# Memory attention: where a pair's second batch is weighted, and what turns the first pair's values and probabilities

## What is computed

```python
xn  = layernorm(x) * ln_g + ln_b              # (32, 512)
q   = split_heads(xn @ Wq)                    # 16 heads of 64
kv  = xn @ Wkv
mem = split_heads(memories @ Wm)              # memories = context, 257 rows
k   = concat([kv[:, :1024] heads, mem])       # 32 + 257 = 289 keys
v   = concat([kv[:, 1024:] heads, mem])       # the same mem is keys and values
attn = softmax(q @ k.T / 8)
out = (attn @ v) @ Wo + bo                    # added to x
```

## Time and profile before

| | us |
|---|---|
| runs of the kernel (3) | 2068.11, 2071.55, 2072.27; median 2071.55 |
| profiled execution, its time | 2070.35 |
| its span, first to last instruction | 2068.6 |
| mean granted TensorE clock | 0.984 |
| PE / DVE / ACT busy | 1985.6 / 1229.0 / 882.2 |
| the loop over pairs | about 1314.8 to 1860 |

### The profile page before, as it was taken

The page is one execution under the profiler, slowest core; times in us unless marked ns, Lnnn a source line. Parts: engine busy times, 40 slices in busy tenths (PEclk is TensorE's granted clock), DMA queues, the critical chain, the costliest instruction groups (busy, mean ns, idle before and its releaser), DMA issues. The chain is left out here.

```text
span 2068.6 us, 34656 instructions
## 1 busy us (share of the span) xinstructions
PE 1985.6 (96%) x14206; PEld 1441.4 (70%) x14206; DVE 1229.0 (59%) x2068; ACT 882.2 (43%) x2075; POOL 61.1 (3%) x78
## 2 busy tenths in 40 slices
PE   7999999899999999989999999899999999989999
PEld 6864455578878888844446788677777777774687
DVE  6446589563356888899999310355444453548563
ACT  4224443353324323589997332233232332333342
POOL 0000000000000000200000000000000000000122
PEclk9999999999999999999999999899999999999999
DMA  7210000131110110120002145566567464643001
GB/s 267 82 49 1 1 2 2 42 107 41 41 42 21 62 42 25 58 102 1 21 1 94 52 139 166 169 181 172 130 185 187 116 191 126 160 159 100 1 1 41
DMA packets 125581, 174.73 MB, mean 84 GB/s; under 512 B 12256, under 2 KB 83936, under 8 KB 124960
## 3 DMA queue, kind: packets, MB, share of 16 engines
q1 hardware_dynamic: 125424, 172.52, 27.9%
HBM read 118.09 MB, written 22.94 MB: 68 GB/s over the span
## 5 line engine op out<-in xcount | busy, mean ns | idle before, releaser
L1307 ACT ACTIVATE R<-bank 128x512 f32<-128x512 f32 (+1 forms) x150 | 89.4, 599 | 393.2 <-PE bank L965 292.2
L1576 ACT ACTIVATE R<-R 128x64 f32<-128x64 f32 x896 | 217.0, 342 | 3.4 <-DVE R L2288 3.4
L962 PE MATMUL bank<-cth,wmh 128*128 128x512 f32 x512 | 207.4, 405 | 5.5 <-ACT arena L1681 4.2
L962 PE MATMUL bank<-cth,wml 128*128 128x512 f32 x512 | 200.7, 392 | 0.0
L532 PE MATMUL bank<-XN,arena 128*128 128x512 f32 x320 | 148.6, 617 | 0.0
L965 PE MATMUL bank<-ctl,wmh 128*128 128x512 f32 x512 | 137.8, 391 | 0.0
L962 PEld LDWEIGHTS bank<-cth,wmh 128*128 128x128 f32 x512 | 96.7, 189 | 39.3 <-issue 19.1
L532 PE MATMUL bank<-Y,arena 128*128 128x512 f32 x256 | 115.9, 597 | 1.7 <-ACT H L1619 1.7
L532 PEld LDWEIGHTS bank<-XN,arena 128*128 128x128 f32 x320 | 61.4, 198 | 72.1 <-issue 71.7
L965 PEld LDWEIGHTS bank<-ctl,wmh 128*128 128x128 f32 x512 | 96.6, 189 | 20.6
L962 PEld LDWEIGHTS bank<-cth,wml 128*128 128x128 f32 x512 | 96.8, 189 | 18.2
(11 more groups left out here) (442 smaller groups left out, 4173.9 us busy)
## 6 DMA issues: line engine op xcount, KB each, us to landing
Y<-value_turn SPq DMA_DIRECT2D x240, 128.0 KB, 2.9
H<-in_ctxT SPq DMA_DIRECT2D x30, 512.0 KB, 5.3
arena<-in_L_attn_mlp_w SPq DMA_DIRECT2D x8, 1024.0 KB, 5.2
probs<-R SPq DMA_DIRECT2D x15, 512.0 KB, 4.0
R<-probs SPq DMA_DIRECT2D x60, 128.0 KB, 3.1
R<-value_rows SPq DMA_DIRECT2D x32, 132.0 KB
arena<-in_L_ffn_Wg SPq DMA_DIRECT2D x4, 1024.0 KB, 6.7
arena<-in_L_ffn_Wu SPq DMA_DIRECT2D x4, 1024.0 KB, 5.3
```

Of the source, the lines that this page charges most:

```text
L962: mm(bank, w_[:, o // 4, k, tl(o % 4)], cth[:, k, :, :], start=(k == 0 and w_ is wmh), stop=False)
L1307: fn(dst, src, ACT.Copy).then_inc(act_bank_free, 1)
L1576: last = fn(into[:, x // 2, h, :, x % 2], RC["Ey"][:, t, h, :], ACT.Copy, scale=RC["Ex"][:, t, h, 8 * j + x:8 * j + x + 1])
```

## The change

Pair 0 is treated as the last pair was: PE transposes its values and the probabilities of both batches, DVE copies them out of the banks, and neither DVE's block transposes nor SP's `move_values` run for it. `move_values` is left for pairs 1 to 14, and its counts move by one pair.

In every pair but the last, `weighted(b1)` moves on PE and DVE: on PE it follows the scores(b0) of the next pair, ahead of unit 2; on DVE it follows maxima(b0) of the next pair. For the last batch it stays where it was.

```diff
+        def at_edge(pr):
+            return pr in (0, PAIRS - 1)
@@ PE, weighted
-                if i == 0 and bb // 2 < PAIRS - 1:
-                    pe.wait_ge(values_full, 256 * (bb // 2 + 1))
-                if i == 0 and bb // 2 < PAIRS - 1:
-                    pe.wait_ge(probs_full, 64 * (bb // 2 + 1))
+                if i == 0 and not at_edge(bb // 2):
+                    pe.wait_ge(values_full, 256 * (bb // 2))
+                    pe.wait_ge(probs_full, 64 * (bb // 2))
@@ PE, loop over pairs
                 attention_scores(b0)
-                if pr == PAIRS - 1:
+                if pr:
+                    weighted(b0 - 1)
+                if at_edge(pr):
                     value_blocks(b0)
...
                 attention_scores(b1)
-                if pr == PAIRS - 1:
+                if at_edge(pr):
                     value_blocks(b1)
...
-                if pr == PAIRS - 1:
+                if at_edge(pr):
                     prob_blocks(b0)
...
                 weighted(b0)
-                weighted(b1)
+            weighted(2 * PAIRS - 1)
@@ DVE, turn_values and turn_probs
-                if pr:
-                    dve.wait_ge(values_full, 256 * pr)
+                if pr > 1:
+                    dve.wait_ge(values_full, 256 * (pr - 1))
...
-                if pr:
-                    dve.wait_ge(probs_spilled, 16 * pr)
+                if pr > 1:
+                    dve.wait_ge(probs_spilled, 16 * (pr - 1))
@@ DVE, loop over pairs
                 maxima(b0)
+                if pr:
+                    weighted(b0 - 1)
                 if pr and pr + 1 < PAIRS:
                     memory(pr + 1, (2,))
-                if pr < PAIRS - 1:
+                if not at_edge(pr):
                     turn_values(pr)
                     turn_probs(pr)
-                else:
-                    dve.wait_ge(values_full, 256 * pr)
+                elif pr:
+                    dve.wait_ge(values_full, 256 * (pr - 1))
                     dve.wait_ge(dve_bank_full, UV.at[("pv", 2 * pr - 1)] + 1)
                     values(b0)
+                else:
+                    dve.wait_ge(act_bank_full, UA.at[("dq", 1, 3, C2 - 1)] + 1)
+                    values(b0)
                 maxima(b1)
-                if pr == PAIRS - 1:
+                if at_edge(pr):
                     values(b1)
...
-                if pr == PAIRS - 1:
+                if at_edge(pr):
                     for blk in range(2):
                         v.tensor_copy(probs_moved[:, :, blk, :].rearrange("p c (g q) -> p g c q", g=4),
                                       unit(("prT", b0, blk))[:, :].rearrange("p (g c q) -> p g c q", g=4, c=4)).then_inc(dve_bank_free, 1)
...
                 weighted(b0)
                 if pr == PAIRS - 1:
                     standardise(4, 0, lambda: weighted(b1))
-                else:
-                    weighted(b1)
@@ SP
             def move_values(pr):
-                sp.wait_ge(values_turned, 4 * (pr + 1))
-                if pr:
-                    sp.wait_ge(dve_bank_full, UV.at[("pv", 2 * pr - 1)] + 1)
+                sp.wait_ge(values_turned, 4 * pr)
+                sp.wait_ge(dve_bank_full, UV.at[("pv", 2 * pr - 1)] + 1)
...
-                if pr < PAIRS - 1:
+                if not at_edge(pr):
                     move_values(pr)
```

More of the change, by code:

```diff
@@ L2806, in move_values @@
             def move_values(pr):
-                sp.wait_ge(values_turned, 4 * (pr + 1))
-                if pr:
-                    sp.wait_ge(dve_bank_full, UV.at[("pv", 2 * pr - 1)] + 1)
+                sp.wait_ge(values_turned, 4 * pr)
+                sp.wait_ge(dve_bank_full, UV.at[("pv", 2 * pr - 1)] + 1)
                 for a in range(4):
[L2812 to L2815, removed]
+                    if a == 2:
+                        sp.wait_ge(probs_turned, 2 * pr)
+                        if pr > 1:
+                            sp.wait_ge(probs_full, 64 * (pr - 1))
                         sp.dma_start(dram["probs"].rearrange("c k j n -> (c k) (j n)"), prob_turn.rearrange("p j b n -> p (j b n)")
@@ L2820, in move_values @@
                                      ).then_inc(values_full, 16)
-                if pr < PAIRS - 1:
[L2822 to L2825, removed]
+                sp.wait_ge(probs_spilled, 16 * pr)
+                for j in range(4):
+                    sp.dma_start(probs_moved[32 * j:32 * j + 32].rearrange("p c b n -> p c (b n)"),
+                                 dram["probs"][:, :, j, :].rearrange("c k n -> k c n")).then_inc(probs_full, 16)
             for pr in range(PAIRS):
```

## The result

The changed kernel has a median of 2059.25 us over 6 runs (2054.74 to 2064.03) against 2071.67 for the kernel before in the same comparison (2068.11 to 2073.91): 12.4 us less by the medians. The ratio is 0.9947, 95% interval 0.9934 to 0.9959, which is 11.0 us less (8.5 to 13.7). In a second comparison (run `e3_after_again`) it was 2056.45 against 2068.43, 12.0 us less; ratio 0.9939 (0.9925 to 0.9953), 12.6 us less. Forecast was 2057, with a range of 2051 to 2065, and 14.1 us less. The profiled execution took 2058.5 us.

What follows compares the result with a forecast made beforehand. TensorE, busy 1985.6 of 2068.6 us, was taken as the bound. Gains of 7.4 (pair 0), 5.8 (order) and 0.9 us (last pair) sum to 14.1, so 2070.35 becomes 2056.3, taken as 2057; range 2051 to 2065.

Steps and rivals of the forecast that it cites:

- Part 1: Pair 0 turned by PE: 5.1 us of added transposes fit into idle time, gain 7.4 us.
- W: Instant when a pair's weighted(b0) begins on PE; for pair 0 forecast at 1333.5 us against 1339.59 before.
- rival 2: Clock still falls in pair 0, as transposes fill the idle time: gain 9.8 us in total, 2061 us, chance 0.12.
- Part 2: Middle pairs, weighted(b1) behind the next scores: instruction-fetch stall falls from 8.0 to 2.2 us, gain 5.8, bounds 0 and 8.
- the 224s: Dense run of 96 + 96 + 32 PE matmuls per pair, before and after the change; its issue stalls are Part 2's gain.
- the latency from crossing to arrival: Middle pairs: PE resumes 2.8 to 3.5 us after crossing into the packet before; 0 to 0.6 us of stall left.
- the issue waits at these two lines: Sign of being right: PE's issue waits at L1066 and L1024, weighting and scores, fall from 9 to 2 or 3 us.
- the waits for R<-probs: PE's waits for moved probabilities: none in pair 0, 4.1 us elsewhere unchanged; growth by what stalls give back means wrong.
- Rival 1: Only the edges gain, as fetch stalls keep their size: gain 8.3 us, 2063 us, chance 0.22.
- Part 3: Last pair: DVE starts values(30) 0.6 us after the dense run instead of 1.55, gain 0.9 us.
- later stages whose packets fall elsewhere: Allowance of 1 to 2 us for stages behind, which takes the range's lower end to 2051 us.
- Rival 3: DVE held at the moved weighting, weighted(b0 - 1): 5.7 us slower at 1 us of delay per pair, 2077 us, chance 0.03.

Runs made afterwards that it cites:

- e3_after_again: The changed kernel run once more, unchanged, for a second profile: median 2056.45 us against 2068.43 for the kernel before, ratio 0.9939.
- e10: The changed kernel with only one of every four PE transposes in pair 0: clock 0.50 for 10.2 us, weighted(0) 21.0 us after the first scores; no total time given.
- e1: The changed kernel with weighted(b1) back right behind weighted(b0), so only pair 0's change remains: 2062.19 us, ratio to the kernel before 0.9976.
- e2: The kernel before with only weighted(b1) moved behind the next pair's first scores: 2061.75 us, ratio to the kernel before 0.9965.
- e9: The kernel before run once more, unchanged, for a second profile: 2062.27 us for that one execution.

## Why the prediction was right, and where it was not

The total was right: 12.4 and 12.0 us less by the medians (11.0 and 12.6 by the ratios) where 14.1 were forecast. But it was so with a compensation of errors: in the profiles only 7.4 us of it lie in the changed part. Pair 0 gave 7.1 us, the middle pairs 5.1, and the last two took 4.8 back (means of two profiles each). The 4 to 5 us that fill the gap were not foreseen and are not explained; to that extent the hit is luck.

- **Part 1, pair 0.** Forecast from the first scores to the first value DMAs of pair 1: 7.4 us. Those DMAs start at 1340.27, 32.2 us after scores(0), against 38.9 before: 6.7. The missing 0.7 is an issue wait of 0.97 behind the dense run. W came 18.6 us after the first scores, 18.7 in the prediction (1333.5 less 1314.8). The cover that hid the 5.1 us of transposes was there as described, and DVE's second maxima began 5.2 us after the scores. The clock stayed up at 1.00, which refutes rival 2, and e10 shows that it was the transposes that kept it there. (The row set against rival 2, 1827 to 1835 us, holds three short gaps of 0.57, 0.24 and 0.78 us, not two.) The Trainium skill (TensorE: Matmul & The Clock Gate, Part 4) says transposes do not count for the clock; the windows of e10 and of the changed kernel say otherwise for these transposes of 128 x 128 in fp32.
- **Part 2, the order.** Right in mechanism, too large in size. The prediction took 8.0 us of stall, of which 2.2 would stay, a gain of 5.8. Its own measure, the issue waits of the 224s, was 8.0 in both profiles of before; afterwards 5.4 and 3.0 are left, and 0.97 and 0.71 behind pair 0's dense run, a gain of 1.6 to 4.3. Measured as excess over 59.6, which takes in pauses too short for the list of waits: 12.3 and 13.0 before, 8.5 and 6.1 after, a gain of 3.8 to 6.9. The term that was mis-sized is the latency from crossing to arrival. I had 2.8 to 3.5 us and took what was left as 0.25 us in nine pairs; in the changed kernel's first profile it was 3.1 to 3.9 us in the middle pairs, so single waits reach 1.05. One of the signs that I had named did not come: the issue waits at these two lines were to fall from 9 to 2 or 3 us, and were 8.8 and 7.1, as the last pair gained what the middle ones lost. Whether the waits for R<-probs outside pair 0 grew by what the stalls gave back is open: 5.8 and 3.7 us, against 4.1 and 1.4 before. Rival 1, only the edges, falls by e1 and e2.
- **Part 3, the last pair.** The step itself held: in e2 DVE starts `values(30)` 0.8 us after the dense run ends, where it took 1.55 before and 0.6 was forecast. What failed is a step that was not there. I costed pair 0's added matmuls by their duration and not by their number. The latter moves the packet edges behind them, and in the last pair one moved from the probability blocks (a 0.24 us wait) into the scores of batch 31, on the chain DVE and ScalarE wait for, while 6 MB of loads were under way: 2.37 us, a clock at half behind it, in all 46.3 and 44.8 us against 41.5 and 40.0. I had put "later stages whose packets fall elsewhere" at 1 to 2 us in the range, and looked for it in the wrong place.
- **What made up for it** is not fully shown. From scores(0) to the end the two profiles each give 7.4 us on average (753.1 less 745.7), the medians 12. The rest lies ahead of scores(0), in unchanged code with stretches of half clock that come and go, or in executions that were not profiled. Mean clocks over the whole span are 0.983 to 0.988 in the 17 timed runs of the kernel before and 0.989 to 0.991 in the 5 of the changed one (e3's comparison); which part of this is pair 0's 13.7 us of half clock removed, and which the last pair's added, two profiles can't tell.
- Rival 3 did not occur: DVE never waited for the moved weighting in the middle pairs.

## What to carry to other kernels

Where PE runs hundreds of short matmuls in a row, count instructions as well as microseconds. Look for "issue" waits that recur every 128 matmul and weight-load pairs, break up the dense run with long matmuls (that removed all but one in the middle pairs here, though it shortened them by only 1.3 us), and keep bulk loads out of its way. An instruction added early moves every later packet edge. So a difference of a few tenths of a per cent between two versions may be the place of the edges: shift them with empty instructions in an idle spot before a change is judged by it.

Idle time of a few microseconds on PE is worth filling with the transposes that would otherwise go by DVE and DMA. They cost nothing in that place, and they held the clock for what follows; what they cost here came 500 us later, by moving the packet edges.

## What the runs showed that I had not expected

- Instruction packets are late under bulk loads: 7.5 us from crossing an edge to arrival with 6 MB of loads under way, 3 to 4 us in the middle pairs. The Trainium skill (Runtime: NRT & Kernel Launch, Instruction fetch mechanics) has packets of 256 instructions, which the shifts by half the added instructions, modulo 128 matmuls, confirm. It calls the cost of crossing mostly hidden. Over the whole span these runs do not deny that (16.7 us of issue waits in 2068.6), but in dense runs of short matmuls they do: single waits reach 1.55 us, in e9.
- The place of the edges alone was worth 5.8 us with the same work (2048.92 with 128 empty instructions against 2054.73 with 64, in one comparison), and up to 7.5 us between two comparisons (2048.92 against 2056.45; as ratios to the kernel before 0.9898 against 0.9939).
- Ahead of the attention, the same code took 1304.6 to 1314.8 us, with 24 to 48 us of half clock in it.
- 192 drains of an idle PE kept it until 14.4 us, 4 us beyond its first data.
